# A new order for ScalarE behind the last attention score, with two sums of roots on VectorE

## The reference

```
denom    = max((1 - |q|^2) * (1 - |k|^2), 1e-6)
cosh_arg = max(1 + 2 * |q - k|^2 / denom, 1)
dist     = arccosh(cosh_arg)
attn     = softmax(-dist);  out = attn @ v;  x = x + out @ wo.T
logits   = layernorm(x) @ Wg + bg
gates    = softmax(logits);  idx = argmax(gates)
h        = gelu(layernorm(x) @ W1[e] + b1[e], exact);  y = h @ W2[e] + b2[e],  e = idx
```

## Time and profile before

| | us |
|---|---|
| median of three runs | 1125.2 |
| lowest and highest run | 1120.56, 1126.07 |
| the profiled execution | 1122.71 |
| its span | 1121.0 |
| TensorE busy | 1039.6 (93%) |
| VectorE busy | 807.4 (72%) |
| ScalarE busy | 791.6 (71%) |
| GpSimd busy | 676.6 (60%) |

### The profile page before, as it was taken

One profiled execution on the slowest core, in us unless ns is written; L12 is line 12 of the kernel. 1 busy time (PEld: TensorE's weight loads), 2 busy tenths in 40 slices (PEclk: granted clock), 3 DMA queues, 4 the chain that ended last, 5 costly groups with the idle time before them and its releaser, 6 DMA issues.

```text
span 1121.0 us, 36561 instructions
## 1 busy us (share of the span) xinstructions
PE 1039.6 (93%) x15373; PEld 775.5 (69%) x15373; DVE 807.4 (72%) x1056; ACT 791.6 (71%) x1452; POOL 676.6 (60%) x613
## 2 busy tenths in 40 slices
PE   3799999999999999999999999999999999766788
PEld 1376777777777777777777777777767777543466
DVE  2788887777777777777777777767777759457442
ACT  3587777777777777777777777777867756798754
POOL 5266666666666666666666666776654546735133
PEclk9999999999999999999999999999999999787699
DMA  8931320000000000000000000003000100000000
GB/s 238 257 74 35 63 55 7 16 7 17 7 17 6 17 8 16 7 17 7 16 7 17 8 16 7 17 7 120 6 3 7 51 28 3 2 1 1 1 1 20
DMA packets 59381, 33.83 MB, mean 30 GB/s; under 512 B 35643, under 2 KB 56147, under 8 KB 59219
## 3 DMA queue, kind: packets, MB, share of 16 engines
q1 hardware_dynamic: 58498, 28.87, 10.2%
q10 hardware_dynamic: 720, 2.62, 0.7%
HBM read 22.57 MB, written 0.52 MB: 21 GB/s over the span
## 4 chain that ended last, share of the span: by engine, by line
PE 81%; DVE 7%; issue 4%; ACT 3%; POOL 2%; DMA 2%; SPq 0%; ACTq 0%; POOLq 0%; DVEq 0%
PE ps L1420 15%; PE ps L1382 14%; PE ps L1502 13%; PE ps L1449 6%; PE ps L1548 5%; PE ps L1543 5%; PE ps L1546 5%; PE ps L1490 4%; PE ps L803 2%; PE ps L763 2%; POOL psums L2082 2%; PE ps L1481 1%; PE ps L1367 1%; PE ps L579 1%; DMA ctx_hi<-spare 1%
## 5 line engine op out<-in xcount | busy, mean ns | idle before, releaser
L2082 POOL TENSOR_TENSOR psums<-probs 128x512 f16<-128x512 f32 x512 | 590.1, 1174 | 328.2 <-ACT probs L1727 274.9
L1718 ACT ACTIVATE probs<-ps 128x512 f32<-128x512 f32 x512 | 279.7, 600 | 193.2 <-PE ps L1502 192.1
L1896 DVE TENSOR_REDUCE m_part<-ps 128x2 f32<-128x1024 f32 x256 | 312.7, 1224 | 139.5 <-PE ps L1449 138.1
L1727 ACT ACTIVATE probs<-probs 128x512 f16<-128x512 f32 x384 | 242.0, 632 | 0.3
L1502 PE MATMUL ps<-q_hi,k_p 64*128 64x256 f16 x2048 | 211.1, 269 | 0.0
L1543 PE MATMUL ps<-v_sb,probs 128*128 128x65 f16 x2048 | 205.3, 192 | 4.5 <-POOL psums L2082 4.4
L1546 PE MATMUL ps<-v_sb,probs 128*128 128x64 f16 x2048 | 205.2, 192 | 0.0
L1548 PE MATMUL ps<-v_sb,psums 128*128 128x65 f16 x2048 | 204.8, 194 | 0.0
L1543 PEld LDWEIGHTS ps<-v_sb,probs 128*128 128x128 f16 x2048 | 188.4, 98 | 19.6 <-POOL psums L2082 6.1
L1546 PEld LDWEIGHTS ps<-v_sb,probs 128*128 128x128 f16 x2048 | 188.0, 97 | 16.0
L1548 PEld LDWEIGHTS ps<-v_sb,psums 128*128 128x128 f16 x2048 | 188.1, 97 | 0.0
(11 more groups left out here) (246 smaller groups left out, 1670.7 us busy)
## 6 DMA issues: line engine op xcount, KB each, us to landing
ctx_hi<-in_L_ffn_W_dram SPq DMA_DIRECT2D x2, 2048.0 KB, 10.1
wqk_raw<-in_L_xattn_w_q_dram SPq DMA_DIRECT2D x16, 128.0 KB, 2.3
wqk_raw<-in_L_xattn_w_k_dram SPq DMA_DIRECT2D x16, 128.0 KB, 2.6
k_p<-in_ctx_dram ACTq DMA_DIRECT2D x4, 512.0 KB, 8.3
wv_raw<-in_L_xattn_w_v_dram SPq DMA_DIRECT2D x16, 128.0 KB, 2.4
wo_raw<-in_L_xattn_w_o_dram SPq DMA_DIRECT2D x16, 128.0 KB, 2.1
ctx_hi<-in_ctx_dram SPq DMA_DIRECT2D x7, 256.0 KB, 5.7
ctx_lo<-in_ctx_dram SPq DMA_DIRECT2D x7, 256.0 KB, 6.4
```

The source lines that it names most:

```text
L1718: nc.scalar.activation(p_raw[:, s:s + 2, h, :], ps[:, score_bank(n, pair, h), :].rearrange("p (k q) -> p k q", k=2), ACT.Exp, scale=XSCALE ...
L1727: nc.scalar.activation(p_hi[:, s % NP, :, :], p_raw[:, s % NX, :, :], ACT.Copy) \
L1896: nc.vector.tensor_reduce(m_part[:, j, t, :], ps[:, bank:bank + 2, :], AX.X, ALU.max) \
L2082: nc.gpsimd.tensor_tensor(p_lo[:, s % NP, :, :].rearrange("p h q -> p (h q)"), p_raw[:, s % NX, :, :].rearrange("p h q -> p (h q)"), p_hi[ ...
```

## The change

On ScalarE the exponentials of groups 0 to 3 stand more closely together, the copies of averages 2 and 3 stand among the roots of group 4, the copy of the turned output (`take_turned(1, 0, ...)`) stands behind the roots of group 6, and the gates stand behind the exponential of group 4. On TensorE the turn of average 3 and the turn of the output stand one unit later, and on VectorE the normalisation too. The sums of roots of groups 6 and 7 move from GpSimd to VectorE, with a semaphore of their own.

```
-AVERAGE_AFTER = {4: (0, None), 6: (1, 0), 8: (2, 1), 9: (3, 2), 10: (None, 3)}
-TURN_AFTER, PROJECT_AFTER, NORMALISE_AFTER = 13, 15, 11
+AVERAGE_AFTER = {4: (0, None), 6: (1, 0), 8: (2, 1), 9: (3, 2), 11: (None, 3)}
+TURN_AFTER, PROJECT_AFTER, NORMALISE_AFTER = 14, 15, 12
...
-            for gg in range(8):
+            for gg in range(6):
                 pool.wait_ge(s_r2, gg + 1)
                 nc.gpsimd.tensor_tensor(ratio[gg], root_of(gg), ratio[gg], ALU.add) \
                     .then_inc(s_ra, 1)
...
             def logarithms(gg):
-                act.wait_ge(s_ra, gg + 1)
+                if gg < 6:
+                    act.wait_ge(s_ra, gg + 1)
+                else:
+                    act.wait_ge(s_rb, gg - 5)
...
             weights(0)
             weights(1)
+            weights(2)
             take_average(0)
-            weights(2)
+            weights(3)
             take_average(1)
-            weights(3)
+            root_of_product(4)
             take_average(2)
-            roots(4)
+            root_of_sum(4)
             take_average(3)
             roots(5)
+            roots(6)
             take_turned(1, 0, OUT_BANKS[0][0])
-            for gg in range(6, 8):
-                roots(gg)
+            roots(7)
             root_of_variance(act, 3, slice(0, 2))
...
+            weights(4)
             gates(0)
-            for gg in range(4, 8):
+            for gg in range(5, 8):
                 weights(gg)
...
+            def sum_of_roots(gg):
+                dve.wait_ge(s_r2, gg + 1)
+                nc.vector.tensor_tensor(ratio[gg], root_of(gg), ratio[gg], ALU.add).then_inc(s_rb, 1)
+
+            sum_of_roots(6)
             residual(0)
             variance(3, slice(0, 2))
             normalised(3, slice(0, 2))
+            sum_of_roots(7)
```

More of the change, by code:

```diff
@@ L334, in perceiver @@
         s_ge = sem("s_ge")
+        s_rb = sem("s_rb")
         s_bt = sem("s_bt")
```

## The result

| | before | after |
|---|---|---|
| median of 22 runs, us | 1122.36 | 1119.80 |
| lowest, highest | 1119.88, 1126.40 | 1115.03, 1122.60 |
| span of the profiled execution | 1121.0 | 1118.7 |
| ratio after to before | | 0.997, interval 0.9962 to 0.9978 |

By the ratio the kernel became 3.4 us faster (2.5 to 4.3; the medians differ by 2.6), clear of noise but within 0.5%: no change by the bound of the forecast. The forecast was 1120.5 us, with 4.1 us off.

A forecast was written before the change was run, and what follows sets the result against it. ScalarE, nearly full from 1005 to 1054 us with 5.9 us idle, was taken as the bound; 2.4 us up to the layer norm's root plus 1.7 at the gates gave 4.1 off, hence 1120.5 us, range 1115.5 to 1125.3.

The forecast's parts named there:

- ScalarE's order: ScalarE from first exponentials to group 7's roots: waits filled by reordering, these roots done at 1031.1 instead of 1033.75 us.
- the head start: About 2.65 us on ScalarE by copy 3 of the averages: three waits, one copy behind a root, and overlaps.
- The sums: Sums of roots 6 and 7 on VectorE: 2.3 us each (bounds 2.1 and 4.5), against 4.52 on GpSimd.
- Cover at the residual: VectorE's sum 6 lies under TensorE's projection, ahead of the residual, with 0.6 us to spare.
- The term for the variance: Residual to layer norm's root: 2.67 us less 0.68 without GpSimd's sum, giving 2.0.
- Sum 6's move: Sum 6 on VectorE ends at 1029.7 us, ahead of the residual at 1030.3; GpSimd's sum 5 holds it to 1027.4.
- The gates: ScalarE's wait of 1.70 us for the logits, ahead of the gates, closes with exponential 4 put first: 1.7 us won.
- (D): Rival: VectorE's sums take 4.5 us each or are locked out that long; gain 2.5 us, time 1122, chance 0.07.
- (B): Rival: TensorE's clock rises 4 us or more later in the program; gain 1.5 to 2, time 1123, chance 0.2.
- (C): Rival: TensorE's work at low clock from 1057 to 1063 runs faster; gain 6 to 7, time 1117.5, chance 0.2.
- (E): Rival: slower than before through a longer low clock in the experts' loop, up to 1130.8 us; chance 0.03.
- The level: Whole-kernel starting time: median of three runs 1125.2, mean of four executions 1123.6; forecast set between their results, 1121.1 and 1119.5.

The follow-up runs named there:

- sums_back: Changed kernel with all eight sums of roots on GpSimd again; table load to last exponential 50.20 us, ratio 1.0002 to the kernel before.
- six_on_pool: Changed kernel with only the sum of roots 6 on GpSimd again; table load to last exponential 46.08 us, against 46.10 in the changed kernel.

## Why the prediction was right, and where it wasn't

**ScalarE's order.** Each time forecast, with the 2.0 us of the later start added, against the trace: first root 1016.2 and 1016.19; copy 3 at 1020.2 and 1020.17; copy of the turned output 1027.8 and 1027.82; roots 7 done 1033.1 and 1033.38; last exponential done 1051.9 and 1051.83. The one difference is unit 15, 0.3 us later, since VectorE reached unit 10 at 1020.45 and not 1020.04. What the order does to the residual is right too, and the sums have no part in it: 28.32 us behind the load before, 26.55 in the changed kernel, 26.53 in sums_back. But the head start was counted as won by the order, with only 0.68 us for the sums. That step failed: sums_back has the order and no gain. The roots come sooner, and so does GpSimd's sum 7, onto the variance.

**The sums.** 2.3 us a sum, measured 2.28. Cover at the residual 0.6, measured 0.54. Root at 1034.3 with the shift, measured 1034.27. The term for the variance, 0.68 us, was the right size but a small part of the matter: in the new order the sums left on GpSimd cost 4.1 us (root at 32.64 against 28.54). In the kernel before, the end of GpSimd's sum 6 set the root, and an order that brings sum 7 ahead of the variance makes that instruction 3.4 us longer still (4.28 against 0.85). The prediction used VectorE's wait as a number to subtract and didn't ask what the other GpSimd sum would hit with a new order. That sum 6 would be held by sum 5 until it ends, as the prediction has it, is right. Sum 6's move, argued at length, is worth nothing (six_on_pool).

**The gates.** The 1.7 us is right for the edit made alone and wrong for the edit here. In the changed kernel the logits come 5.25 us sooner relative to the load (37.36 against 42.61) and the table only 2.45, which alone removes the wait. The prediction had both numbers, logits at 1041.4 and table in at 1042.5, and should have seen that the gates needn't move. The total was right since the wait is gone either way, and was counted once.

**The rivals.** (D) fell, the sum being 2.28 us. (B)'s condition came true and its price didn't. The clock rose later in the program (the granted clock averages 0.59 from 1048 to 1050 us before, but only 0.73 from 1050 to 1052 after, though the last exponential ends 2.1 us sooner in that trace), and the averages of groups 4 and 5 took 1.94 us each. TensorE before, and after:

```profile
1048.70 1.51 PE L723 MATMUL ps<-v_sb,psums 128*32 128x256 f32 x16
...
1050.45 1.07 PE L723 MATMUL ps<-k_p,psums 128*32 128x256 f32 x16
```

```profile
1046.37 1.94 PE L724 MATMUL ps<-v_sb,psums 128*32 128x256 f32 x16 [0.85 <-ACT v_sb L938]
...
1048.76 1.94 PE L724 MATMUL ps<-k_p,psums 128*32 128x256 f32 x16
```

But these run beside ScalarE's exponentials, and the first masked product came 4.5 us sooner, not less than 3. For (C) and (E) the loop's length speaks: 61.4 us before and after, so neither shows in these two traces. The clock does move it, by 1.8 us between two executions of the changed kernel and by up to 3.4 over all kernels, with no tie to the change in these traces. The 4.14 us of the stretch lie within the interval that the runs give, 2.5 to 4.3; the runs don't tell them from 3.4.

**The level.** Three runs gave a median of 1125.2, 22 gave 1122.36. I leant on the mean of all executions for half the way, so the forecast set out from 1124.6, 2.2 us too high, and took 4.1 off where the medians fell by 2.6. That it came out 0.7 us above the result is in part luck; the 46.10 us of the stretch are not.

## What to carry to other kernels

An instruction of two columns on VectorE can last as long as the sum that GpSimd happens to be on, if it is of a kind that waits for it (here the variance's TENSOR_SCALAR and the Newton product's TENSOR_TENSOR): before moving an engine's work earlier, list what GpSimd will be doing at each short VectorE step of the critical chain. When two edits are priced, look whether both remove the same wait; each alone then has a price and the second has none. Where runs scatter by more than the gain, count from an event just ahead of the change to one just behind it: that gave 46.10 and 46.08 for two executions whose spans differ by 3 us.

## What was not expected of the hardware

Not every VectorE instruction waits for GpSimd. The variance and the Newton product, two columns each, waited until GpSimd's sum ended, to within 0.04 us (4.28, 3.93, 3.42, 1.25, 0.96 us long instead of 0.16 or 0.17). In the trace before, the residual (0.69 us), the statistics (0.75) and their aggregation (0.25) took under sum 6 what they take without it, and so did, under sum 7, the reciprocal just ahead of the Newton product:

```profile
1035.03 0.17 DVE L1848 RECIPROCAL rstd<-rstd 128x2 f32<-128x2 f32 x1 [0.34 <-ACT rstd L847]
```

The other way round the wait looks shorter, in one trace. GpSimd's added sum, with VectorE's 2.2 us ahead of it, ran from 1030.86 to 1036.52, 1.14 us over its usual 4.52, and so not held for the whole 2.2 us, as far as GpSimd's spans can be read. Whether it shares for a while, or prepares during the wait, stays open. The Trainium skill, page "SBUF — State Buffer", section "Who interferes with whom", calls the shared port pair an exclusive lock and lets the order of issue decide who blocks. For VectorE the traces agree; for GpSimd this one shows a wait, but not the full one.
